# An attention kernel followed by routed experts: GpSimd's eight row stores of a batch taken apart and placed between its other work

## The reference

```python
def reference(L0_attn_x, ...):            # x: 16 batches of 512 tokens of 128 features
    mod = (_silu(L0_c) @ L0_wmod).reshape(L0_c.shape[0], 6, 1, -1)
    sa, ca, ga, sb, cb, gb = (mod[:, 0], ..., mod[:, 5])
    h = _layernorm(x, axis=-1) * (1 + ca) + sa
    x = x + ga * _L0_attn_ref(h, Wq, Wk, Wv)
    h = _layernorm(x, axis=-1) * (1 + cb) + sb
    x = x + gb * _L0_ffn_ref(h, w1, b1, w2, b2, w3, b3, gate_w)
    return x

# _L0_attn_ref: 16 heads of 8 features
    Q = (x @ Wq.T).reshape(H, b, s, dkh)      # K and V likewise
    atten = softmax(einsum('hbqd,hbkd->hbqk', Q, K))
    out = einsum('hbqk,hbkd->hbqd', atten, V).reshape(b, s, -1)
    y = out + x
    return (y - mean(y, axis=(1, 2))) / sqrt(var(y, axis=(1, 2)) + EPS)

# _L0_ffn_ref: each token goes to the 2 best of 8 experts
    top_vals, top_idx = top_k(x @ gate_w, 2);  gate_scores = softmax(top_vals)
    h = silu(x @ w1[e] + b1[e]) * (x @ w2[e] + b2[e])      # 128 -> 256
    out = sum over the two e of gate_score * (h @ w3[e] + b3[e])
```

## Time and profile before

| | us |
|---|---|
| median of 3 runs (1115.34 to 1119.27) | 1115.79 |
| span of the profiled execution, first to last instruction | 1191.7 |
| PE busy | 993.4 |
| DVE busy | 912.5 |
| ACT busy | 816.4 |
| POOL busy | 664.7 |

### The profile page before, as it was taken

The page is one execution under the profiler, slowest core; times in us unless marked ns, Lnnn a source line. Parts: engine busy times, 40 slices in busy tenths (PEclk is TensorE's granted clock), DMA queues, the critical chain, the costliest instruction groups (busy, mean ns, idle before and its releaser), DMA issues. The chain is left out here.

```text
span 1191.7 us, 19302 instructions
## 1 busy us (share of the span) xinstructions
PE 993.4 (83%) x5725; PEld 373.4 (31%) x5725; DVE 912.5 (77%) x1983; ACT 816.4 (69%) x1555; POOL 664.7 (56%) x1061
## 2 busy tenths in 40 slices
PE   4699979898998989989999898888888865888780
PEld 2122222222222222222232222222145643655550
DVE  6788889987989989998998978998635734444667
ACT  2138888887877888877887777888756743565640
POOL 3833045565675656856667565364346556566562
PEclk9999999998989999999998989999689978999995
DMA  8758766664556656565555654332322433343456
GB/s 202 143 127 250 151 154 159 133 132 142 109 152 126 133 137 125 155 130 123 147 117 151 118 128 116 87 99 72 110 60 85 159 121 107 110 131 116 136 175 229
DMA packets 369049, 159.63 MB, mean 134 GB/s; under 512 B 290656, under 2 KB 333552, under 8 KB 365232
## 3 DMA queue, kind: packets, MB, share of 16 engines
q1 hardware_dynamic: 347376, 122.06, 44.7%
q0 software_dynamic: 9088, 18.76, 4.6%
q10 hardware_dynamic: 12480, 17.57, 4.2%
HBM read 87.85 MB, written 71.82 MB: 134 GB/s over the span
## 5 line engine op out<-in xcount | busy, mean ns | idle before, releaser
L1246 DVE TENSOR_REDUCE neg_max<-bank 128x1 f32<-128x512 f32 x1024 | 643.1, 680 | 86.9 <-PE bank L1979 73.9
L1755 ACT ACTIVATE probs<-bank 128x512 f32<-128x512 f32 x1024 | 545.3, 605 | 119.4 <-PE bank L1991 91.9
L1979 PE MATMUL bank<-Kt,Qt 48*128 48x512 bf16 x1024 | 348.4, 405 | 72.1 <-DVE neg_max L1246 51.9
L1991 PE MATMUL bank<-Qt,Kt 51*128 51x512 bf16 x1024 | 344.4, 401 | 13.4 <-ACT probs L1755 11.7
L2004 PE MATMUL bank<-probs,Vt 128*16 128x512 f32 x2048 | 283.6, 627 | 0.0
L1137 POOL DMA_INDIRECT y_dram<-y_rows,row_in x156 | 153.4, 983 | 99.6 <-DVE y_rows L1646 57.7
L1979 PEld LDWEIGHTS bank<-Kt,Qt 48*128 48x128 bf16 x1024 | 75.4, 94 | 418.5 <-DVE neg_max L1246 345.8
L1062 POOL DMA_INDIRECT rows_dram<-rows,slot x128 | 127.0, 992 | 45.5 <-issue 32.6
L1883 ACT ACTIVATE probs<-bank,w3b_cur 128x512 f32<-128x512 f32 x78 | 52.8, 687 | 99.0 <-PE bank L2080 45.4
L1639 DVE SCALAR_TENSOR_TENSOR probs<-bank,w3b_cur,probs 128x512 f32<-128x512 f32 x78 | 58.2, 748 | 69.8 <-ACT probs L1883 54.4
L2078 PE MATMUL bank<-ht_first,w_cur 128*128 128x512 f32 x156 | 71.1, 456 | 40.5 <-ACT w_cur L1869 24.5
(11 more groups left out here) (234 smaller groups left out, 1228.0 us busy)
## 6 DMA issues: line engine op xcount, KB each, us to landing
o_dram<-o_sb ACTq DMA_DIRECT2D x64, 256.0 KB, 3.0
row_in<-rows_dram SPq DMA_DIRECT2D x39, 260.0 KB
Qt<-q_dram SPq DMA_DIRECT2D x64, 128.0 KB
Kt<-k_dram SPq DMA_DIRECT2D x64, 128.0 KB
y_in<-y_dram SPq DMA_DIRECT2D x16, 512.0 KB
q_dram<-q_parts SPq DMA_DIRECT2D x48, 128.0 KB, 4.8
k_dram<-k_parts SPq DMA_DIRECT2D x48, 128.0 KB, 5.5
rows_dram<-rows SPq DMA_DIRECT2D x4, 1040.0 KB, 5.7
```

The costliest lines, as they stand in the source:

```text
L1246: dve.tensor_reduce(neg_max[:, side, a, col:col + 1], score_a[m % 3][:], AX_X, ALU.max, negate=True).then_inc(s_max, 1)
L1755: act.activation(probs[:, 4 * (j % 2) + (k ^ 1)], score_b[n % 3][:], ACT.Exp).then_inc(s_exp, 1)
L1979: pe.matmul(score_a[m % 3][:], Qt[b % BUFS][first:first + ROWS, n, P * c:P * c + P], Kt[b % BUFS][first:first + ROWS, n], start=True, stop ...
L1991: pe.matmul(score_b[m % 3][:], Kt[b % BUFS][first:first + ROWS + PARTS, n, P * c:P * c + P], Qt[b % BUFS][first:first + ROWS + PARTS, n], ...
```

## The change

For batches 0 to 11, whose rows are stored in stages 4 to 15, all eight stores move into stage f+4, as single ones. They stand after `split_max(b - 1, 1)`, after `f_move`, directly behind it once more, this one with a wait of its own until VectorE has done 12 maxima of the stage, after `front_rows`, after `add_h`, after `split_max(b, 0)`, after `gap` and after `gap_one`. For batch 12 both runs of four stand one after the other in stage 16. Batch 13's first run stays at the end of stage 16. In stages 3 to 13 `split_k` goes from behind `split_q` to a place behind `split_max(b, 0)` and ahead of `gap`.

```diff
+            def scatter_tile(f, i, quad=None):
+
+                if quad is not None:
+                    pool.wait_ge(s_max, (f + 4) * STEPS + 4 * quad)
+                k, t = i // TT, i % TT
+                pool.indirect_dma_start(rows_dram, bass.IndirectOffsetOnAxis(ap=slot[:, k, t:t + 1], axis=0),
+                                        rows[:, f % 2, k, t], None).then_inc(s_scattered[f % 2], DMA)
+
             def stage(b, par):
+
+                def row_tile(i, quad=None):
+                    if has(b, 4, NB - 1):
+                        scatter_tile(b - 4, i, quad)
+
                 if has(b, 1, NB):
                     split_max(b - 1, 1)
+                row_tile(0)
                 if has(b, 0, NB - 1):
                     relay_v(b, par)
                 if has(b, 3, NB):
                     f_sums(b - 3)
                     front_power(b - 3)
                     f_move(b - 3)
-                if has(b, 4, NB):
+                row_tile(1)
+                row_tile(2, 3)
+                if b == NB:
+                    scatter(b - 4, 0)
                     scatter(b - 4, 1)
                 if has(b, 3, NB):
                     front_rows(b - 3)
+                row_tile(3)
                 if has(b, 2, NB + 1):
                     add_h(b - 2)
+                row_tile(4)
                 if has(b, 1, NB - 3):
                     split_q(b + 2)
+                if has(b, 1, 2):
                     split_k(b + 2)
...
+                row_tile(5)
+                if has(b, 3, NB - 3):
+                    split_k(b + 2)
                 if has(b, 3, NB):
                     gap(b - 3)
+                row_tile(6)
+                if has(b, 3, NB):
                     front_hits(b - 3)
                     gap_one(b - 3)
+                row_tile(7)
...
                     front_slots(b - 3)
+                if b == NB:
                     scatter(b - 3, 0)
```

## The result

The changed kernel takes 1153.9 us (median of 4 runs, 1150.1 to 1155.9) beside 1115.6 for the kernel before (4 runs, 1106.4 to 1119.3). The ratio is 1.0345 (95% interval 1.0317 to 1.0373): slower by 38 us. I had forecast 1120.8 in a range of 1099 to 1127, with a chance of 0.32 for slower. The recorded execution is one of the changed kernel's four runs, the shortest, and took 1150.1 us.

The account below looks back on a forecast made before the run. VectorE was taken to set the pace in the attention part, TensorE up to three tiles ahead. The gap wait's +5.2 and stage 16's -0.2 made +5.0 on 1115.8, so 1120.8 us, in a range of 1099 to 1127.

Parts of the forecast that it names:

- the terms of `split_max` and `gap`: GpSimd's `split_max(b, 0)` 1.1 us sooner, counted zero; `top_gap` behind three more stores and K's split, done at 512.52.
- The term for the gap wait: ScalarE's `gap_exp` waits 0.80 us for `top_gap`; 0.52 pass in each of ten stages, +5.2 us, bounds 0 and 24.
- the gap wait passes whole, and more: Rival at ScalarE's `gap_exp`: 8 us over ten stages, 13 with stores of 1.5 us, so 1124 to 1129; chance 0.15.
- The hold: TensorE's results arrive two or three us late at runs of four stores; doubted for timed runs, so breaking runs counted nothing.
- The hold is real: Rival: timed runs have the hold at runs of stores too, so 19.5 us are saved, 1101.3, down to 1099; chance 0.30.
- the 1177: Sign: the changed kernel's profiled span falls to about 1177 without holds over 1 us at stage turns, while the median doesn't follow.
- The rule on trace records: The block carrying trace records pushes back and can throttle an engine; by it broken runs gain nothing in timed runs, otherwise 19.5 us.

Follow-up runs that it names:

- y_stores_spaced_b: The kernel before with a short GpSimd memset between the expert part's stores of y, attention part untouched; 1.0000 of the kernel before, which took 1119.0 us.
- changed_again: The changed kernel, unchanged, run and recorded again beside the kernel before at 1213.6 us; ratio 0.9868.
- gap_before_k: The changed kernel with only `top_gap` put ahead of K's split; 0.9752 of the kernel before, in later groups 0.9642 and 1.0055.
- k_split_fitted: The changed kernel with `top_gap` ahead of K's split, whose first subtraction waits for VectorE's first write of `coded`; 1.0001 of the kernel before, in another group 0.9636.
- stores_paired_b: The kernel before with each run of four stores cut into two pairs, nothing else moved; 1.0008 of the kernel before, which took 1119.0 us.
- before_again: The kernel before, unchanged, recorded a second time; 1191.8 us, in a group where its median was 1189.0 us.

## Why the prediction was wrong

**The sum, as the runs have it.** Against the kernel before's attention part without holds, as y_stores_spaced_b has it (47.18 us a stage in stages 4 to 14, and 48.1 for stage 3), the changed kernel needs 49.92 and 49.8: 11 x 2.74 + 1.7 = 31.8 us. VectorE's small operations make 2.15 - 0.62 = 1.53 us in each of ten stages, and as much in stage 3, 17 us. Six stages in which the clock falls are 51.2 - 48.9 = 2.3 us longer each, 14 us. Together 31, for a recorded run that was the shortest of its four. That the others had more such stages is an inference, from two of their mean clocks (0.940 and 0.942, beside 0.947 in the recorded run and in the fourth) and from the nine in changed_again.

**The step that failed first** is in the terms of `split_max` and `gap`: K's split "as before", moved at no cost. I priced GpSimd's operations by what waits for them, and none by what runs beside them. The split came from VectorE's rounds 7 and 8 into the end of round 8 and round 9, where four of VectorE's operations read two operands from SBUF. Moved alone, the split costs 1.35%, 15 us of 1116 (there it holds `y_dev` and `tied`, 1.55 us a stage). In the changed kernel 1.10 of the 1.53 us are `tied` and `coded` beside the split; 0.42 are `y_dev` beside a lone store with K's split directly behind it. I had put this at nothing for VectorE, too. With `top_gap` behind the same store, in gap_before_k and k_split_fitted, `y_dev` takes 0.21 to 0.25 us, so most of the 0.42 goes with the split's place as well. The order of both engines was there to be laid side by side. The Trainium skill's page SBUF — State Buffer, in the same section "SBUF: two separate sides" that I cited, has the rule: VectorE and GpSimd share a port pair, an operation of VectorE with two SBUF inputs needs it against one of GpSimd that reads SBUF, and whichever starts first has it for the whole instruction. The traces agree: beside K's split a held operation ends 0.01 to 0.08 us after the operation of GpSimd that it began beside. I took that section for its sentence on DMA and passed over the one that speaks against this change.

**The term for the gap wait** (+5.2) had the right wait and the wrong consequence. I expected 1.9 us of idle time ahead of `gap_exp`, released by `top_gap`; it was 1.7. Of this I let 0.52 pass. At the full clock nothing passes: stage 8 is 48.9 us, and 47.3 (a stage of y_stores_spaced_b from the fifth on) with VectorE's 1.53 makes 48.8. At the lower clock 2.3 pass. With 2.20 us of idle time, stages 4 to 14 became 3.58 us longer each (558.4 against 519.0, by 11). With `top_gap` ahead of K's split, three profiles in three groups show no stage from 4 to 14 with a slow round 11. It is not the only way to the lower clock, since stores_paired_b has it in stages 4 and 12 without such a wait (ScalarE is idle for 1.5 us there, behind its own issues, as in other stages where the clock stays). My rival "the gap wait passes whole, and more" had the place and the side but ended at 1129, as its price grew with the store's length and not with the clock.

**The hold.** That recording brings it about is refuted: y_stores_spaced_b is recorded with runs of four and has none, and before_again has holds in a group whose timed runs took 1189 us as well. "The hold is real" is true in one condition and not in the other. In the long one the four in a row cost 560.0 - 520.0 = 40 us in stages 4 to 14, twice the 19.5 that I had for them, and even the changed kernel comes out 1.1 to 1.3% ahead. Part of it is the lower clock behind the holds. The 0.96 of the earlier trace rows, which I said explains little, is a mean that hides rounds at 0.50. By what a run of stores holds the engines is not shown. Where the kernel before takes 1116, as in the result, there is nothing to give back. So zero was right for the timed runs by luck, for a wrong reason: the trace of before came from the other condition. The 75.9 us between its span and the median split as the windows show: 551.50 - 519.0 = 32.5 in stages 4 to 14, and in the part behind attention 364.3 - 322.4 = 41.9, in the first traces of before and after:

```profile
827.40:1191.70 364.30, 271.20 (x1159) 169.03 (x1156) 188.68 (x410) 189.09 (x313) 201.34 (x231) 0.87 0.42 130
```

```profile
825.90:1148.30 322.40, 264.48 (x1159) 165.66 (x1156) 189.47 (x409) 189.38 (x313) 207.62 (x233) 0.88 0.47 147
```

The rule on trace records that I cited from the Trainium skill's page NOTIFIC — the notification-queue block is needed for none of this.

**Points that held.** No hold in the changed profile, and its span fell while the median didn't follow. It fell to 1148.3, though, and not to the 1177 that I had named, since the part behind attention was 41.9 us shorter too, in the short condition. `y_stats` waits for nothing, and a lone store costs GpSimd 1.0 us without making another engine wait, but for the two beside `y_dev` and ahead of `top_gap`. k_split_fitted has all eight and equals the kernel before.

**A better version** is the kernel before with its fours cut into pairs: as fast as the kernel before in the short condition (1.0008) and ahead of it in the long one (0.9632). k_split_fitted does as well (1.0001 and 0.9636). Both beat the changed kernel in either.

## What to carry to other kernels

Where an operation of GpSimd is moved, list what VectorE does at its new time and look for two-operand SBUF operations; the price was the remainder of GpSimd's operation, each time. A wait put into ScalarE is not over when it catches up, if TensorE stands meanwhile: read the granted clock of the next rounds. And when the span and the median of one kernel are 6% apart, suspect two conditions: take the order of things from the rows, and a wait only once a second recording agrees.

## What the hardware did that I had not expected

- The same kernel on the same chip (5) took 1213.6 us in one group of runs and 1116.0 in another. Where it is long, the expert part is some 40 us longer and runs of four stores hold the other engines for 1 to 3 us; pairs and lone stores don't. What sets the condition stays open.
- `y_dev` is held beside a lone store, or not, by something other than its start. In three recordings of the changed kernel it begins 0.31 to 0.35 us into a store of 1.01, takes 0.60 to 0.66 us and ends about 0.05 before the store does. In five recordings of gap_before_k and k_split_fitted it begins 0.30 to 0.35 into the same store and takes 0.20 to 0.26. What differs is GpSimd's next instruction: the first cast of K's split in the one, the small `top_gap` in the other. Why that should matter while the store still runs is not shown.
- A cast of GpSimd holds VectorE for its remainder as a subtraction does: the second write of `coded` in k_split_fitted, 483 ns in place of 191.
